# Two PSUM copies moved from ScalarE to VectorE, and a chunk's output stage emitted inside the next chunk's middle stage

## The reference

```python
xn = layernorm(x)                                   # x: 16 x 2048 x 2048, f32
# branch s: a small recurrent block on xn
u  = layernorm(xn) @ W_in + b_in                    # 2048 -> 8
h  = scan(h[t] = sigmoid(decay_logit) * h[t-1] + u[t])
x2 = xn + h @ W_out + b_out + layernorm(xn) * D_skip
s  = x2 + relu(layernorm(x2) @ W_down + b_down) @ W_up + b_up
# branch g: an 8-bit fake-quantized dense layer on xn
y  = relu(quant(xn, per row) @ quant(kernel, per column) + quant(bias))   # 2048 x 2048
g  = silu(quant(y, per row))
out = x + s * g
```

## Time and profile before

| | us |
|---|---|
| median of 2 runs | 2327.41 (2324.85 to 2329.98) |
| the profiled execution | 2327.71 |
| its span on the slowest core (core 7) | 2326.1 |
| spans of the 8 cores | 2319.9 to 2326.1 |
| busy PE / DVE / ACT / POOL | 1384.2 / 1080.0 / 702.7 / 298.7 |

### The profile page before, as it was taken

How to read it: one execution, slowest core, us unless ns; L and a number is a source line. 1 busy time by engine, 2 the same in 40 slices (tenths; PEclk the granted TensorE clock), 3 DMA queues, 4 the chain that set the end, 5 groups by cost and what they waited for, 6 DMA issues and landing times.

```text
span 2326.1 us, 28140 instructions; the slowest of 8 cores (2319.9 to 2326.1 us)
## 1 busy us (share of the span) xinstructions
PE 1384.2 (60%) x5025; PEld 609.5 (26%) x5025; DVE 1080.0 (46%) x2791; ACT 702.7 (30%) x804; POOL 298.7 (13%) x132
## 2 busy tenths in 40 slices
PE   0343343356666666666666666666666666666664
PEld 0222222222222222222222222222222222222221
DVE  4333333354444444555444544445544444444442
ACT  0211211123333333333333333333333333333332
POOL 0000000001111111111111111111111111111111
PEclk9999999996666676666666666666666666666666
DMA  1112111201111111111111111111111111111110
GB/s 22 48 37 55 37 44 47 55 1 37 37 37 37 37 37 37 37 37 37 37 37 37 37 37 37 37 37 37 37 37 37 37 37 37 37 37 42 41 37 28
DMA packets 56496, 86.55 MB, mean 37 GB/s; under 512 B 11118, under 2 KB 44014, under 8 KB 52206
## 3 DMA queue, kind: packets, MB, share of 16 engines
q1 hardware_dynamic: 56348, 84.75, 12.2%
HBM read 51.17 MB, written 33.55 MB: 36 GB/s over the span
## 4 chain that ended last, share of the span: by engine, by line
DVE 35%; PE 29%; issue 16%; ACT 13%; POOL 3%; DVEq 2%; SPq 1%; ACTq 0%; DMA 0%; POOLq 0%
PE py L706 13%; DVE x2tmp L608 4%; DVE x L609 4%; POOL s L793 3%; PE pb L409 3%; PE pb L375 3%; DVE st L472 3%; PE pb L570 3%; ACT xn L468 3%; DVE s L684 3%; DVE t L449 3%; DVEq L73 2%; DVE kstat L384 2%; DVE t L723 2%; ACT g L788 1%
## 5 line engine op out<-in xcount | busy, mean ns | idle before, releaser
L706 PE MATMUL py<-kq,ixqT 128*128 128x512 bf16 x2048 | 588.0, 458 | 39.3 <-DVE x L609 34.7
L793 POOL TENSOR_TENSOR s<-g,s 128x1024 f32<-128x1024 f32 x64 | 150.0, 2343 | 2006.4 <-ACT g L788 1862.1
L706 PEld LDWEIGHTS py<-kq,ixqT 128*128 128x128 bf16 x2048 | 231.5, 114 | 405.5 <-issue 255.4
L510 PE MATMUL pb<-eyef,xn 128*128 128x128 f32 x512 | 137.7, 373 | 191.9 <-DVE xnT L514 155.3
L633 ACT ACTIVATE sqscr<-x 128x512 f32<-128x512 f32 x128 | 80.8, 631 | 394.7 <-DVE x L609 394.7
L456 ACT ACTIVATE st<-nw 128x2 f32<-128x2 f32 x32 | 6.6, 206 | 575.4 <-DVE nw L455 575.4
L797 POOL TENSOR_TENSOR o<-s,x 128x1024 f32<-128x1024 f32 x64 | 149.8, 2341 | 17.5 <-POOL s L793 17.5
L510 PEld LDWEIGHTS pb<-eyef,xn 128*128 128x128 f32 x512 | 82.5, 161 | 253.2 <-issue 225.7
L527 PE MATMUL pb<-eyeb,qbf 128*128 128x128 bf16 x512 | 125.8, 265 | 10.1 <-ACT qbf L482 1.7
L412 DVE CAST kq<-pb 128x512 bf16<-128x512 f32 x64 | 44.3, 692 | 161.1 <-PE pb L409 161.1
L472 DVE TENSOR_REDUCE st<-xn 128x1 f32<-128x2048 f32 x32 | 73.2, 2286 | 79.3 <-ACT xn L468 79.3
(11 more groups left out here) (174 smaller groups left out, 1855.5 us busy)
## 6 DMA issues: line engine op xcount, KB each, us to landing
x<-L_attn_x SPq DMA_DIRECT2D x32, 1024.0 KB, 6.6
out<-o SPq DMA_DIRECT2D x64, 512.0 KB, 3.0
xn<-L_ffn_kernel SPq DMA_DIRECT2D x128, 64.0 KB, 2.3
s<-L_ffn_kernel SPq DMA_DIRECT2D x128, 64.0 KB, 2.4
wint<-L_attn_W_in SPq DMA_DIRECT2D x16, 4.0 KB
wdnt<-L_attn_W_down SPq DMA_DIRECT2D x16, 16.0 KB
x<-L_attn_W_up SPq DMA_DIRECT2D x1, 256.0 KB
eyef<-c_eye_f SPq DMA_DIRECT2D x1, 64.0 KB
```

What stands on the lines that cost most here:

```text
L510: tlast = T(deps, lambda e, j=j, b=b, bank=bank, xn=xn: e.transpose(bank[:, 128 * b:128 * (b + 1)], xn[:, 128 * j:128 * (j + 1)], eyef[:]) ...
L706: mmlast = T(deps, lambda e, j=j, qq=qq, fofs=fofs, ixb=ixb: e.matmul(py[qq][:], ixb[:, 128 * j:128 * (j + 1)], kq[:, D * j + fofs:D * j + ...
L793: sg = G([e4, rc["s1"], rc.get("tap_s")], lambda e, h=h: e.tensor_tensor(sb_[:, 1024 * h:1024 * (h + 1)], g_t[:], sb_[:, 1024 * h:1024 * ( ...
```

## The change

The two ACT copies of T2 become DVE copies. `emit_mid` is cut in two: its first part, T1 and T2 with their evacuations, keeps the name; the rest, from `augT` on, is `emit_midb`. In the loop, the second-half evacuation and the output stage of chunk c-1 are emitted between these two parts of chunk c, instead of after `emit_pro(c)`; for the last chunk they are emitted after the loop.

```diff
-                if g < 2:
-                    t2e.append(V([tlast, dep_ix_free],
-                                 lambda e, g=g, ixb=ixb, bank=bank: e.tensor_copy(ixb[:, 512 * g:512 * (g + 1)], bank[:])))
-                else:
-                    t2e.append(S([tlast, dep_ix_free],
-                                 lambda e, g=g, ixb=ixb, bank=bank: e.activation(ixb[:, 512 * g:512 * (g + 1)], bank[:], AF.Identity, bias=0.0, scale=1.0)))
+                t2e.append(V([tlast, dep_ix_free],
+                             lambda e, g=g, ixb=ixb, bank=bank: e.tensor_copy(ixb[:, 512 * g:512 * (g + 1)], bank[:])))
...
+            rc["t1e"] = t1e
             if TRUNC == 22:
                 rc["last"] = [t2e[3], t1e[3]]
+            return
+
+        def emit_midb(c):
+            rc = R[c]
+            if "last" in R[c]:
                 return
...
             dep_prow = R[c - 1].get("rm2e") if c >= 1 else None
             dep_prow2 = R[c - 1].get("s1") if c >= 1 else None
             rc["augT"] = T([rc["inv0"], dep_prow, dep_prow2, L["eyef"]],
...
             for c in range(NCH):
                 emit_mid(c)
+                if c >= 1:
+                    emit_big_evacs(c - 1, 1)
+                    emit_echunk(c - 1)
+                emit_midb(c)
                 emit_big_half(c, 0)
                 emit_mid2(c)
                 emit_big_evacs(c, 0)
...
                 emit_big_half(c, 1)
                 if c + 1 < NCH:
                     emit_pro(c + 1)
-                emit_big_evacs(c, 1)
...
-                emit_echunk(c)
+            emit_big_evacs(NCH - 1, 1)
+            emit_echunk(NCH - 1)
```

More of the change, by code:

```diff
@@ L540, in emit_mid @@
             rc["ixb"] = ixb
+            rc["t1e"] = t1e
             if TRUNC == 22:
                 rc["last"] = [t2e[3], t1e[3]]
+            return
+        def emit_midb(c):
+            rc = R[c]
+            if "last" in R[c]:
                 return
+            st = st_t[c % 2]
+            nw = nw_t[c % 2]
+            nwi = nwi_t[c % 2]
+            xn = xn_t[c % 2]
+            nwd = rc["st0"]
+            t1e = rc["t1e"]
+            t2e = rc["t2e"]
+            ixb = rc["ixb"]
             dep_prow = R[c - 1].get("rm2e") if c >= 1 else None
```

## The result

The changed kernel takes 2561.91 us (median of 9 runs, 2561.02 to 2595.79) beside 2327.77 us for the kernel before (median of 8) on the same chip: a ratio of 1.1014, with a 95% interval of 1.0996 to 1.1031. One of the nine runs, 2595.79 us, was slow on one die; the ratio is over the fast runs, and so differs a little from the quotient of the two medians (1.1006). The changed kernel is 234 us slower. The forecast was 2561 us.

What follows compares the result with a forecast made beforehand. The chunk loop was taken to be bound by a chain of hand-offs, with no engine near full. 31 x 7.54 = +234 us on the profiled 2327.7 us gave 2561 us, range 2512 to 2598.

Steps and rivals of the forecast that it cites:

- The chain end to end: Before `auge`: transposes, second evacuation, scale and output chain, formerly overlapped, run in series; +7.54 us a chunk, +234 us, chance 0.87.
- the last copy's start at +12.1: Fourth T2 evacuation on DVE: starts 12.1 us after the start of L472, lasts 0.69 us, read from chunk 0.
- L789 at +15.95: Start of ACT's output chain (L779 before): 15.95 us after L472 starts, 0.2 us behind the scale at +15.75.
- `auge` at +24.55: ScalarE copy behind the whole 8.61 us output chain: starts 24.55 us after L472 starts, against +17.0 before.
- ACT's new wait of about 8 us: Sign expected in the profile: the output chain's first activation waits for DVE by about 8 us a chunk.
- DVE's of about 10: Sign expected in the profile: DVE idle for about 10 us ahead of `r1a`.
- This edit alone removes 0.96 us ahead of `auge`: Moving T2 copies 2 and 3 off ACT: `auge` 0.96 us earlier, 2 x 0.69 us added to DVE.
- POOL's additions follow the activations as before: POOL's additions in the output stage: same place behind the activations, listed under what costs nothing.
- I take the mean, zero: Phase of the clock's rise inside the big matmul: -40 to +28 us in all possible, counted as zero.
- The hidden output chain: Rival: `auge` and `r1T` get past the activations, DVE limits; 2.15 us less a chunk, 2261 us, chance 0.04.
- this rival: T1/T2 transposes gain from a warmer TensorE clock: up to 1.5 us a chunk, 46 us, giving 2515; chance 0.07.
- the estimate of 2535: Total if 16 transposes at the upper clock save 0.8 us a chunk, 26 us, by the skill's gap formula.

Runs made afterwards that it cites:

- Experiment three: Changed kernel with `augT`, `auge`, `r1T`, `r1a` moved from `emit_midb` to the end of `emit_mid`, ahead of the output chain: 2170.93 us, ratio 0.9322.
- experiment two: Changed kernel with copies 2 and 3 of T2 back on ACT, so only the order differs from the kernel before: 2517.28 us, ratio 1.0811.
- experiment one: Kernel before with only the two T2 copies moved from ACT to DVE, order unchanged: 2314.38 us, ratio 0.9942.
- experiment nine: Changed kernel with `uc` reading its input from PSUM and three more DVE copies of `u_sb` ahead of the product `um`: 2565.51 us, ratio 1.1013.
- run 4: Not a numbered run; "the run 4 us" means the run won 4 us: changed kernel without POOL's last addition of x, 2558.04 us, ratio 1.0999.

## Why the prediction was right

**The chain end to end.** The step that carried the forecast held in each piece: the last copy's start at +12.1 (12.13), L789 at +15.95 (15.96), `auge` at +24.55 (24.59), ACT's new wait of about 8 us (8.31), DVE's of about 10 (9.71), 7.54 us a chunk (7.52). `r1T` waits 12.2 us a chunk where about 11 were forecast. Experiment three shows that the place of `auge` and the three small operations behind it is the cause, and experiment two that the copies, harmless before, add to it.

**The copies.** "This edit alone removes 0.96 us ahead of `auge`": 0.98 in experiment one.

**"POOL's additions follow the activations as before", at no cost.** This step failed. They do follow as before, but it was `auge` that came 0.96 us closer to them, and with it the chain of small DVE steps. `uc` moved under the last addition: +0.95 us a chunk, 29 us. I counted the work behind `auge` as unchanged because none of its instructions changed; its place against POOL did. The sign was to be had in the kernel before, where the same 8x128 step has a minimum of 0.273 and a maximum of 0.760 us.

**"I take the mean, zero" for the clock.** The mechanism named was the right one, the size was off: -0.66 us a chunk, 20 us. The chunk of the changed kernel is held at a length at which the clock rises within 0.65 us of one place every time.

**The x2 passes.** From the start of the first to the start of the last, 0.3 us shorter in all kernels that have all four copies on DVE (5.88 to 5.91) but one, experiment nine (6.02); 6.18 to 6.19 before and in experiment two. The forecast had nothing for it. L601 waits for the last copy; with the copy on DVE, that may be one semaphore less to wait for. This is argued, not shown.

So the agreement to 1 us is partly luck: three terms of +29, -20 and -9 us were missing and cancel. The range would have held each of them.

**The rivals.** The hidden output chain (2261) is not what happened, but it is what the edit could have been: experiment three (2171 us). The transposes did not gain from the clock, because it was not up. They came closer to the big matmul, 7.9 us after L472 instead of 9.3, and yet over the transposes of the steady chunk of the changed kernel (columns as in the earlier trace rows) it was

```profile
1509.49:1513.64 4.15, 3.93 (x17) 1.68 (x17) 2.07 (x3) 0.00 (x0) 0.00 (x0) 0.50 0.00 0
```

and 0.50 in chunks 1 to 30 of both kernels. 16 transposes took 4.15 us and their copies came 1.06 us apart, as before. So the condition of this rival did not come about, and the estimate of 2535 from the Trainium skill's gap per matmul was not put to the test by the change (31 x 0.81 is 25, not 26, so it should read 2536). That the level makes no difference to this block rests on chunk 0 alone, 4.12 us at 1.00.

## What to carry to other kernels

In a kernel whose engines run their queues in order, look for the smallest instruction that others wait for, and ask what stands ahead of it on its own engine: here a 0.25 us copy behind an 8.6 us chain cost 7.5 us a chunk, and its move ahead of the chain won 391 us. Emitting a stage "between" two others does not hide it by itself: what the rest of the later stage waits for must not stand behind it on its own engine. Here moving four small operations ahead of it was enough. And when a chain is shifted, look at what its small steps newly run beside, even where none of them has changed.

## What the runs showed of the hardware

- A DVE step from SBUF to SBUF of 0.27 us (scalar operation), 0.21 us (cast) or 0.47 us (scan) that started while a POOL instruction ran was held until about its end: 1.36, 2.04 and 1.13 us. With an operand in PSUM it was not (0.34 us for the scalar operation, 0.69 us, as always, for an x2 pass in experiment three).
- A loop can be held at a length by TensorE's clock. Four kernels, whose last x2 pass started 38.21, 38.76, 39.13 and 39.44 us after L472, all had a mean chunk of 64.85 to 64.87 us (from chunk 3 on), and their chunks lie within 1.0 us; those of the others wander by 1.7 to 2.4 us. Within such a hold a saving of 0.9 us a chunk on the path won 0.8 us in 30 chunks, and the run 4 us of an expected 33. The time of such a kernel alone doesn't tell whether an edit did something; the time between two marks ahead of the big matmul does.
